# Third layer of a fused four-layer kernel: a round's two chunks of expert rows are gathered at steps 14 and 21 of the round, not both at step 18

## What is computed

```python
topk_scores, topk_idx = jax.lax.top_k(gate_probs, TOP_K)
...
out = jnp.einsum('ted,te->td', expert_out, combine)
```

```python
scores = scores + gc[:, :, :, None] - gc[:, :, None, :]
probs = jax.nn.softmax(scores.astype(jnp.float32), axis=-1).astype(q.dtype)
return jnp.einsum('bhqk,bkhd->bqhd', probs, v)
```

## Time and profile before

| what | value |
|---|---|
| median of 3 runs | 3052.97 us (3048.3 to 3058.53) |
| the profiled execution, its time | 3049.67 us |
| its span (first to last instruction) | 3047.9 us, mean granted clock 0.946 |
| busy: PE, DVE, ACT, POOL | 2587.0, 2064.8, 1794.2, 866.6 us |
| indirect gathers of L830 | 128, mean 982 ns, 56 of them in the third layer |

### The profile page before, as it was taken

One profiled execution on the slowest core, in us unless ns is written; L12 is line 12 of the kernel. 1 busy time (PEld: TensorE's weight loads), 2 busy tenths in 40 slices (PEclk: granted clock), 3 DMA queues, 4 the chain that ended last, 5 costly groups with the idle time before them and its releaser, 6 DMA issues. The chain is left out here.

```text
span 3047.9 us, 77204 instructions
## 1 busy us (share of the span) xinstructions
PE 2587.0 (85%) x30488; PEld 1921.3 (63%) x30488; DVE 2064.8 (68%) x6099; ACT 1794.2 (59%) x3611; POOL 866.6 (28%) x876
## 2 busy tenths in 40 slices
PE   5757799997789999999989999999998657999965
PEld 5645477775456656666666666666665446999943
DVE  5744544444566678666776687667865478999998
ACT  1223355553355666666666666667664468888885
POOL 2224300000212232223223232223211244333377
PEclk9958999998799999999999999999999678999987
DMA  6100144444000000000000000000000003655511
GB/s 201 33 15 30 42 146 145 154 145 121 14 6 16 16 15 8 11 16 16 13 5 16 16 12 5 16 16 13 12 2 12 6 33 116 201 195 200 184 40 45
DMA packets 104452, 175.86 MB, mean 58 GB/s; under 512 B 16417, under 2 KB 73377, under 8 KB 103969
## 3 DMA queue, kind: packets, MB, share of 16 engines
q1 hardware_dynamic: 95904, 154.13, 16.7%
q0 software_dynamic: 8192, 16.79, 1.9%
HBM read 131.15 MB, written 26.74 MB: 52 GB/s over the span
## 5 line engine op out<-in xcount | busy, mean ns | idle before, releaser
L1949 POOL TENSOR_TENSOR l_rinv<-l_ssm,w_neg_half 128x8 f32<-128x8 f32 x128 | 210.0, 1640 | 598.5 <-DVE l_ssm L2234 598.4
L252 PE MATMUL bank<-l_kT,l_qT 32*128 32x128 f32 (+1 forms) x3072 | 357.8, 352 | 5.7 <-DVE l_qm L1316 3.4
L252 PE MATMUL bank<-l_qm,l_kT 32*128 32x128 f32 (+1 forms) x3072 | 354.5, 349 | 2.4 <-DVE l_qm L2145 0.5
L271 DVE TENSOR_REDUCE l_tops<-bank 128x2 f32<-128x256 f32 (+1 forms) x384 | 196.2, 511 | 165.5 <-PE bank L252 149.9
L1979 ACT ACTIVATE l_probsT<-bank 128x768 f32<-128x768 f32 x256 | 207.9, 812 | 168.5 <-PE bank L252 163.8
L2612 DVE RECIPROCAL l_rden<-l_den 128x256 f32<-128x256 f32 x128 | 223.9, 1749 | 31.8 <-ACT l_den L2539 24.3
L830 POOL DMA_INDIRECT back<-sorted_y,pos x128 | 125.7, 982 | 399.1 <-DMA sorted_y<-l_y_tile 365.9
L272 DVE TENSOR_REDUCE l_tops<-bank 128x2 f32<-128x512 f32 (+1 forms) x384 | 227.5, 592 | 0.0
L149 POOL TENSOR_TENSOR l_rstd<-l_var,w_neg_half 128x2 f32<-128x2 f32 (+1 forms) x56 | 42.0, 750 | 632.2 <-DVE l_var L144 632.2
L252 PEld LDWEIGHTS bank<-l_kT,l_qT 32*128 32x128 f32 x3072 | 207.8, 191 | 13.3 <-DVE l_qm L1316 4.9
L252 PEld LDWEIGHTS bank<-l_qm,l_kT 32*128 32x128 f32 x3072 | 205.3, 189 | 5.0 <-DVE l_qm L2145 4.3
(11 more groups left out here) (337 smaller groups left out, 7255.1 us busy)
## 6 DMA issues: line engine op xcount, KB each, us to landing
l_expert<-in_experts SPq DMA_DIRECT2D x72, 768.0 KB, 4.0
l_expert<-in_experts SPq DMA_DIRECT2D x72, 578.0 KB, 3.5
l_x_tile<-sorted_x SPq DMA_DIRECT2D x144, 64.0 KB, 4.1
sorted_y<-l_y_tile SPq DMA_DIRECT2D x144, 64.0 KB, 3.7
l_v_half<-l_v SPq DMA_DIRECT2D x32, 264.0 KB, 3.2
sorted_x<-x_all SPq DMA_DIRECT2D x18, 256.0 KB
l_v_half<-l_v SPq DMA_DIRECT2D x32, 132.0 KB, 3.2
l_x<-in_x SPq DMA_DIRECT2D x8, 256.0 KB, 4.2
```

The source lines that it names most:

```text
L252: lasts.append(pe.matmul(bank[:, at:at + n * P], lhs[:, c * P:(c + 1) * P], rhs[:, x0 * P:(x0 + n) * P], start=False, stop=(i == 1), skip_ ...
L271: dve.tensor_reduce(tops[:, 0, :], two[:, :, 0:s], AX.X, ALU.max)
L1949: pool.tensor_tensor(rinv[:, i, :], ssm[:, i, :], g.neg_half[:, 0:LH], ALU.pow).then_inc(rinv_ready[l], 1)
```

## The change

The two chunks get a place each. The first (index 0 of `GATHER_AT`) is gathered when POOL's list comes to `xnT`, step 14; the second when it comes to `wide_q 1`, step 21. The wait for the chunk's buffer stays with each.

```diff
+GATHER_AT = (("xnT", ), ("wide_q", 1))
...
-                        elif item == ("wide_k", 1):
-                            for c in range(NC * n + GB, min(NC * (n + 1) + GB, CH)):
+                        elif item in GATHER_AT:
+                            c = NC * n + GB + GATHER_AT.index(item)
+                            if c < CH:
                                 gather_pool(pool, g, s, ybuf, gathered, c)
```

## The result

| what | before | after |
|---|---|---|
| median of the runs | 3052.97 us (5 runs, 3045.51 to 3060.89) | 3031.32 us (5 runs, 3022.68 to 3037.78) |
| ratio, 95% interval | | 0.9925, 0.990 to 0.995 |
| the profiled execution | 3049.67 us, span 3047.9 | 3023.43 us, span 3021.6, clock 0.944 |

The median became 21.7 us lower; the forecast was 15.7 us.

A forecast was written before the change was run, and what follows sets the result against it. Bound: at step 18 a PE to ACT to PE chain whose signals come late while POOL writes gather lists. Prices 0.6 + 0.5 replace 2.41 us, saving 1.3 in 12 rounds, 15.7 us: 3037 us, range 3027 to 3055.

The forecast's parts named there:

- Where the time lay: Third-layer gathering rounds, step 18: four gathers make PE's signals late, all 2.41 us between the starts of L1763 and L1700.
- The queue's place, not the step: POOL's queue: what counts is POOL's own order of work, not the step's number; no size given.
- Price at step 18: Second chunk's pair, at the old place of the four: late PE signals cost 0.6 us a round (0.4 to 1.15).
- Price at step 14: First chunk's pair, behind qk 1 1: lateness of L1873's signal goes fully onto the round, 0.5 us (0 to 1.8).
- the right lower row: Lower bound for step 14: a fourth-layer long matmul ends inside a gather and ACT starts 0.03 us later; lateness 0.
- Sum: Rounds 1 to 12: 1.1 us in place of 2.41, 1.3 saved each, 15.7 us in all; chance 0.62.
- The cover: Step 14: POOL keeps 2.4 us idle before qk 1 2; SP's copies and the gathered rows are used only later.
- A: Each gather costs 0.6 us wherever it stands; 2.35 to 2.5 a round, 3052 to 3054 us; chance 0.2.
- B: A pair holds everything until 1.10 us after its end; 3.45 us a round, 3065 us, slower; chance 0.08.
- C: At step 14 DVE stands still while each list is written; 2.6 us a round, 3055 us; chance 0.05.
- the prediction's row: Fourth layer: beside gathers of 1.00 us DVE's reciprocal takes 1.74 us, neither longer than usual; cited against the exclusive lock.
- D: POOL is late enough to issue both chunks together again, so the change does nothing; 3053 us; chance 0.02.

The follow-up runs named there:

- e1: Changed kernel with the chunks at steps 18 and 21, so four gathers start in a row; 2988.86 us (kernel before 2985.09), again 3046.66 us (before 3054.6).
- f1: Second pair behind local 1 1, plus different extra POOL work at step 18's old place in most rounds, against the kernel before; 3047.1 us beside 3054.6.
- v2: Changed kernel with the second pair moved behind the last shift of local 1 1, against the kernel before; 3018.2 us against 3054.6, ratio 0.9872.
- c2: Kernel before with the second pair at another place each round, first at step 14, all four together in rounds 10 and 12; 3038.15 us beside 3049.03.
- e3: Changed kernel with the long matmul of qk 1 2 cut into eight, against the kernel before; 3006.96 us beside 2985.09, again 3062.65 beside 3054.6.
- e2: Kernel before with the second pair at another place each round, all four together in rounds 10 and 12, in a comparison without late signals; 2986.11 us beside 2985.09.
- c1: The changed kernel again, unaltered, as a control against the kernel before; 3030.2 us against 3049.03, ratio 0.9938.
- f3: Matmul of qk 1 2 split into 2 to 16 parts, with and without the pair beside it, plus extra gathers; 3003.68 us, kernel before 2990.6.

## Why the prediction was right, point by point

**Where the time lay: right.** The whole 2.41 us lay between L1763 and L1700, and it went from there. Rounds 13 and 14 are as before (96.21), rounds -1 and 0 still issue four in a row.

**The queue's place, not the step: right, and shown** by e1 (98.63 to 98.67 although steps 18 and 21 are written down for the two chunks).

**Price at step 18: forecast 0.6, measured 0.63, and the number was luck.** L1991 was expected 0.66 behind L263 and came 0.69 behind; L1764 to L1701 was expected as 4.1 us and is 4.19. But the price is that of L1764's signal, 0.65 late where 0.03 is usual: behind it everything runs as in the round without gathers (0.83 and 0.82 from L1988 to L1991). The forecast had this signal, but priced it at only 0.4, its lower bound, because it let L1989 follow L1986 at once; ACT waits 0.22 us between the two even in the round without gathers. The lateness then chosen for L263 filled that gap. f1 gave 1.0 for such a pair at this place in round 2, with L263's signal 1.11 late (1038.49 to 1039.60), and in the changed kernel's own round 2 it is 0.83 (97.60, and 96.77 in v2).

**Price at step 14: forecast 0.5, measured 0 to 0.02.** This is the term that was mis-sized. ACT's L2039 came 0.11 behind L1874 where 0.10 is usual. I named the right lower row, the one long matmul in the earlier trace rows, and then moved up from it because of L1763, whose signals come from several short ones. The row of the same kind should have stood alone: in c2 the same long matmul was on time beside four gathers, and L1880 was on time inside the second gather; in e3 the product was 0.95 late when it was split in eight and ended inside a gather. The whole matmul ended in the gap between two gathers in both timelines shown, so they do not say what its own signal does inside one.

**Sum.** 0.6 + 0.5 in place of 2.41 made 1.3 a round; it is 1.79, so 21.5 us and not 15.7. With the mis-sized term at 0 the same sum gives 1.8.

**The cover: right.** POOL kept 2.43 us idle before `qk 1 2` (2.4 forecast), and nobody waited for SP's copies or for the gathered rows.

**The rivals.** A (so much for each gather) falls: at the place of step 18 one gather costs 0.02, two 0.6 to 1.0, four 2.4, and the same pair costs 0 to 0.63 by place. B (everything is held until 1.10 after a pair) falls: at step 14 L1874's signal came before the pair had ended. Something of it is true in the runs of four: the signal at 1531.39 came 1.09 after the end of the last. C (DVE stands still while a list is written) falls: DVE is busy 70.04 us in the round with gathers and 70.05 without, and the pair at step 14 costs nothing. The Trainium skill (SBUF — State Buffer, section "SBUF: two separate sides") has an exclusive lock there, but for DVE operations of certain kinds only: in a two-port mode, or with two SBUF inputs against a GpSimd operation that reads SBUF. Whether the reciprocal of the earlier trace rows or the rotation is one, no run here shows, so the prediction's row spoke against the rival and not against that rule. One thing stays unexplained: the fourth gather at step 14 (round 10 of c2 and of e2) took 1.40 us where the three before it took 0.94 to 1.03, beside DVE's L2241, an operation on two SBUF tensors that took its usual 0.68. D falls by POOL's timeline.

**What stays open.** Why signals are late in some comparisons and not in others; whether the number of small matmuls or the moment at which they end counts; by what path a gather on POOL holds a signal of PE; and why four gathers of 64 rows hold a signal longer than four of 128. The three comparisons meant for the second were all quick. All experiments but c1 and v2 ran once in a comparison.

## What to carry to other kernels

Where POOL writes lists for indirect transfers, put few of them in a row, and put them where nobody waits at once for PE's signals; beside long matmuls they were free here. A pair cost 0 to 1.0 us by its place, four in a row 2.3 to 7.5, the larger part of the 7.5 as a slower clock. Find the places by giving each round of an unrolled loop another one and comparing the rounds' lengths with a round that has none. Such a price can be there in one comparison and gone in another, so time a change of this kind on more than one chip.

## What the runs showed of the hardware that I had not expected

- **Two levels of the same kernel.** Each comparison ran on one chip. One chip came twice, quick both times (2985.09 and 2986.19 us); the others came once, so it is not shown that the level belongs to the chip. e1 took 2988.86 and 3046.66 us. By windows the difference is 28.7 us before 975.51 and 1004.22, which holds the second layer's scatters, 28.3 in the rounds (1154.95 and 1183.21), and 0.7 in all that follows (856.64 and 857.37).

- **Indirect transfers are what counts.** Four plain transfers from the same queue cost 0.02 us, four indirect ones 2.4 to 6.05.
- **A slower clock came behind a late signal.** In f1's round 7 PE was busy only 1.16 of the 4 us in which it waited for it, and then ran at 1.2 GHz (0.50) for some microseconds before it was back at 2.4 (a granted clock of 0.69 over the next 4 us, 1.00 after that):

```profile
1530.00:1534.00 4.00, 1.16 (x11) 0.54 (x13) 0.67 (x3) 2.61 (x8) 0.30 (x1) 0.96 0.04 11
1534.00:1538.00 4.00, 3.65 (x39) 2.82 (x36) 1.26 (x5) 2.09 (x6) 0.00 (x0) 0.50 0.01 4
```

  PE was busy 92.92 us in that round and 90.12 in round 6: 2.8 of the 6.05 us are slower matmuls. In c2's round 10 the clock was 0.51 for 13.9 us right behind the wait (1797.13 to 1811.00). That the wait brings it on is not shown: f3's round 9, a quick one with 104.74 us, had a clock of 0.50 from 1676.00 to 1684.00 though PE had been busy at least 3.31 us of every 4 before it.
